# A fused two-layer decoder: weights of the first cross attention loaded a stage earlier, clearing and loads moved behind first rows, matrix products placed in waits

## The reference, cut to what matters

```python
x = x + L0_attn(_layernorm(x))            # 16 heads of 64, causal softmax, biases
x = x + L0_xattn(_layernorm(x), ctx)      # 16 heads of 16, softmax over 361 keys
x = x + L0_ffn(_layernorm(x))             # mixture: 2 of 8 experts of 704, and a shared one of 352
x = x + L1_attn(_layernorm(x))            # 16 heads of 16, linear: no softmax
x = x + L1_xattn(_layernorm(x), ctx)      # 16 heads of 64, softmax over 361 keys
x = x + L1_ffn(_layernorm(x))             # mixture: 8 of 64 experts of 128, and a shared one of 256
```

## Time and profile before

| | us |
|---|---|
| median of three runs | 3454.67 |
| the three runs | 3448.93, 3454.67, 3457.12 |
| the profiled execution, as timed | 3452.34 |
| its span in the trace | 3450.6 |
| busy: PE, PEld, DVE, ACT, POOL | 3254.7, 2422.0, 1887.5, 1646.8, 783.8 |

### The profile page before, as it was taken

One profiled execution on the slowest core, in us unless ns is written; L12 is line 12 of the kernel. 1 busy time (PEld: TensorE's weight loads), 2 busy tenths in 40 slices (PEclk: granted clock), 3 DMA queues, 4 the chain that ended last, 5 costly groups with the idle time before them and its releaser, 6 DMA issues. The chain is left out here.

```text
span 3450.6 us, 76147 instructions
## 1 busy us (share of the span) xinstructions
PE 3254.7 (94%) x24554; PEld 2422.0 (70%) x24555; DVE 1887.5 (55%) x5145; ACT 1646.8 (48%) x4614; POOL 783.8 (23%) x854
## 2 busy tenths in 40 slices
PE   8999999899999989899998989999999999998992
PEld 6777776566666656677776766777777777766871
DVE  4655555577777756122222664666666666663433
ACT  4555555566666611122222326666666666652220
POOL 1000000000000000333332110132332332336774
PEclk9999999899999989999999999999999999999996
DMA  8500000400000051211112100010000000025784
GB/s 274 151 0 0 0 0 0 157 9 11 11 11 11 5 161 43 77 30 31 30 29 46 52 0 5 16 43 21 18 14 11 15 13 12 13 81 141 203 221 137
DMA packets 136407, 181.28 MB, mean 53 GB/s; under 512 B 36156, under 2 KB 108601, under 8 KB 135308
## 3 DMA queue, kind: packets, MB, share of 16 engines
q1 hardware_dynamic: 84112, 133.96, 12.6%
q0 software_dynamic: 45760, 26.67, 4.8%
q10 hardware_dynamic: 6460, 19.66, 1.5%
HBM read 116.11 MB, written 103.61 MB: 64 GB/s over the span
## 5 line engine op out<-in xcount | busy, mean ns | idle before, releaser
L1269 DVE TENSOR_REDUCE e_nmx<-PS 128x1 f32<-128x361 f32 x416 | 221.3, 532 | 343.4 <-PE PS L1117 337.5
L1622 ACT ACTIVATE b_p<-PS,b_nmx 100x361 f32<-100x361 f32 x512 | 267.1, 568 | 148.4 <-DVE b_nmx L1704 148.4
L1117 PE MATMUL PS<-e_cT,e_qT 128*128 128x361 f32 x832 | 333.4, 483 | 0.0
L893 POOL DMA_INDIRECT slot_rows<-r_row,r_rows_now x256 | 256.7, 1003 | 336.7 <-DVE e_p L1276 290.2
L1221 ACT ACTIVATE e_pT<-PS 121x384 f32<-121x384 f32 (+1 forms) x416 | 199.0, 479 | 220.9 <-PE PS L1124 220.8
L2637 PE MATMUL PS<-c_wgu,c_tile_xT 128*128 x912 | 291.2, 463 | 1.4 <-ACT c_tile_xT L2692 1.4
L1704 DVE TENSOR_REDUCE b_nmx<-PS 100x1 f32<-100x361 f32 x512 | 243.5, 525 | 44.6 <-PE PS L1468 44.6
L1124 PEld LDWEIGHTS PS<-ident,e_p 128*121 128x121 f32 x1248 | 198.0, 184 | 96.2 <-ACT e_pT L1221 0.4
L1226 ACT ACTIVATE e_p<-PS,e_nmx 128x361 f32<-128x361 f32 x416 | 232.4, 559 | 36.3 <-DVE e_nmx L1269 36.2
L1475 PEld LDWEIGHTS PS<-ident,b_p 100*121 100x121 f32 x1536 | 188.5, 185 | 61.2 <-ACT b_pT L1606 31.0
L1475 PE MATMUL PS<-ident,b_p 100*121 100x100 f32 x1536 | 223.5, 280 | 6.5 <-ACT b_pT L1606 4.4
(11 more groups left out here) (338 smaller groups left out, 6462.9 us busy)
## 6 DMA issues: line engine op xcount, KB each, us to landing
f_w<-in_f_W SPq DMA_DIRECT2D x64, 384.0 KB, 3.7
slot_rows<-a_empty SPq DMA_DIRECT2D x1, 21504.0 KB, 65.3
f_xg<-slot_rows SPq DMA_DIRECT2D x64, 336.0 KB, 3.9
c_wgu<-in_c_GU ACTq DMA_DIRECT2D x8, 1408.0 KB, 16.6
sum<-X SPq DMA_DIRECT2D x2, 3200.0 KB, 57.0
f_sums<-sum SPq DMA_DIRECT2D x16, 400.0 KB
b_cT<-in_ctx_T SPq DMA_DIRECT2D x32, 181.5 KB, 2.3
e_cT<-in_ctx_T SPq DMA_DIRECT2D x32, 181.5 KB, 2.3
```

The costliest lines, as they stand in the source:

```text
L893: pool.indirect_dma_start(out=self.rows, in_=self.row[:, u, :], in_offset=None, out_offset=bass.IndirectOffsetOnAxis(ap=self.rows_now[:, u ...
L1117: sr.fill_done(pe.matmul(sr.at(f"s{m}", ROWS, CTX), qT[:, at:at + ROWS], cT[:, u, 0:CTX], start=True, stop=True), f"s{m}")
L1269: dve.tensor_reduce(nmx[:, m:m + 1], sr.at(f"s{m}", ROWS, CTX), AX.X, ALU.max, negate=True).then_inc(max_ready, 1)
L1622: sr.move_done(act.activation(p[:, g % 2, a, 0:CTX], sr.at(f"s{g}{a}", S, CTX), ACT.Exp, bias=nmx[:, g, a:a + 1]), f"s{g}{a}")
```

## The change

The change has five parts.

First, the weights, the first two contexts and their semaphores of `tiled_cross_attention` move into a class `TiledWeights`, placed on the right side of the on-chip memory. SP issues their six loads at the end of its program in `self_attention`, behind the wait for `slots_cleared`.

Second, in `tiled_cross_attention` POOL does the first root and waits for the two normalised batches before it clears v and p; the waits for `prepared` on PE and DVE move behind the first scores; ACT's eight loads of `c_wgu` are spread over the start of the stage (`load_ahead`). In `packed_cross_attention` POOL makes the routing's constants behind the first normalised pair.

Third, in `dispatch_and_shared` DVE takes the statistics of batches 4 to 6, then normalises pairs 0 and 1, and only then does the statistics of 7 to 15 and the variances of 4 to 15.

Fourth, the loads of experts 4 to 7 of `c_wd` move from step 35 to the start of `tiled_experts`, where SP issues them once the first gather has landed, ahead of `behind.load`.

Fifth, `keep_busy` puts products of the identity with itself, whose result nobody reads, on PE at the start of six stages: 6 in a_, 8 and 4 in b_, 9 in `dispatch_and_shared`, 18 in `tiled_experts`, 11 in d_ and 8 in e_.

The six removed lines at 1396 to 1401 are those of `load` and are cut here.

```diff
...
+def keep_busy(pe, k, bank, n):
+    for _ in range(n):
+        pe.matmul(k.PS[:, bank, 0:128], k.ident[:], k.ident[:], start=True, stop=True)
 def layer_norm_rstd(pool, ln, t):
     pool.wait_ge(ln.var_ready, t + 1)
-def self_attention(k, w):
+def self_attention(k, w, behind):
...
                 sp.wait_ge(k.slots_cleared, 16)
+                behind.load(sp)
...
                             project("k", 1, i)
+                keep_busy(pe, k, 7, 6)
                 turn(-1, False, True)
...
                 layer_norm_rstd(pool, ln, 0)
+                pool.wait_ge(ln.xn_ready, 2)
                 r.make_constants(pool)
                 layer_norm_rstd(pool, ln, 1)
                 pool.wait_ge(loaded, LOADED)
...
                             mr.pass_over_in(pe, i, *[name for name, at in routed.items() if at == n])
+                keep_busy(pe, k, 5, 8)
                 pe.wait_ge(loaded, LOADED)
                 pe.wait_ge(prepared, PREPARED)
-def tiled_cross_attention(k, w, name, ahead_to, ahead_from, ahead_loaded):
-    nc, X = k.nc, k.X
+class TiledWeights:
+    LOADED = 4 * 16
+    def __init__(self, k, ctx, w, name):
+        def sb(n, shape):
+            return ctx.enter_context(k.nc.sbuf_tensor(f"{name}_{n}", shape, F32, side="right"))
+        self.k, self.w, self.name = k, w, name
+        self.wq, self.wk = sb("wq", [128, KC, D]), sb("wk", [128, D])
+        self.wv, self.wo = sb("wv", [128, D]), sb("wo", [128, KC, D])
+        self.cT = sb("cT", [128, 2, 363])
+        self.loaded = k.sem(f"{name}_loaded")
+        self.ctx_loaded = [k.sem(f"{name}_ctx_loaded{u}") for u in range(2)]
+    def load(self, sp):
+        w, loaded = self.w, self.loaded
+        sp.dma_start(self.wq[:], w["Wq"].rearrange("(c p) n -> p c n", p=128)).then_inc(loaded, 16)
+        sp.dma_start(self.wk[:], w["Wk"]).then_inc(loaded, 16)
+        for u in range(2):
+            sp.dma_start(self.cT[:, u], self.k.ctx_T[u]).then_inc(self.ctx_loaded[u], 16)
+        sp.dma_start(self.wv[:], w["Wv"]).then_inc(loaded, 16)
+        sp.dma_start(self.wo[:], w["Wo"].rearrange("(t p) n -> p t n", p=128)).then_inc(loaded, 16)
+def tiled_cross_attention(k, tiled, ahead_to, ahead_from, ahead_loaded):
+    nc, X, name = k.nc, k.X, tiled.name
...
-        wq, wk = sb("wq", [128, KC, T * 128]), sb("wk", [128, T * 128])
-        wv, wo = sb("wv", [128, D]), sb("wo", [128, KC, D])
+        wq, wk, wv, wo, cT = tiled.wq, tiled.wk, tiled.wv, tiled.wo, tiled.cT
-        cT = sb("cT", [128, 2, KEYS * CH])
...
-        loaded, prepared, parity_made = sem("loaded"), sem("prepared"), sem("parity_made")
-        ctx_loaded = [sem(f"ctx_loaded{u}") for u in range(2)]
+        loaded, ctx_loaded = tiled.loaded, tiled.ctx_loaded
+        prepared, parity_made = sem("prepared"), sem("parity_made")
...
                 mr.wait_full(sp, "v02", -1)
                 sp.dma_start(cT[:, 0], k.ctx_T[2]).then_inc(ctx_loaded[0], 16)
                 with sp.Fori(0, TURNS - 2) as i:
-            LOADED = 64
+            LOADED = tiled.LOADED
             PREPARED = 2
             @block.gpsimd
             def _(pool):
+                layer_norm_rstd(pool, ln, 0)
+                pool.wait_ge(ln.xn_ready, 2)
                 pool.memset(v[:], 0.0).then_inc(v_cleared, 1)
                 pool.wait_ge(v_cleared, 1)
                 pool.memset(v[:, :, :, :, A:A + 1], 1.0).then_inc(prepared, 1)
                 pool.memset(p[:, :, :, CTX:KEYS * CH], 0.0).then_inc(prepared, 1)
-                with pool.Fori(0, TURNS + 1) as t:
+                with pool.Fori(1, TURNS + 1) as t:
                     layer_norm_rstd(pool, ln, t)
             @block.tensor
...
+                keep_busy(pe, k, 6, 8)
                 pe.wait_ge(loaded, LOADED)
-                pe.wait_ge(prepared, PREPARED)
                 mr.pass_over(pe, "v10", "v12")
                 turn_x(-1)
+                keep_busy(pe, k, 6, 4)
                 keys(0, 0, -1)
                 mr.pass_over(pe, "r0", "t0")
                 queries(-1)
...
                 values(0, 0, -1)
                 scores(1, 0)
                 values(0, 2, -1)
+                pe.wait_ge(prepared, PREPARED)
                 for a in range(TILES_R):
                     turn_probs(0, a, 0)
                 keys(1, 0, -1)
             @block.scalar
             def _(act):
-                act.wait_ge(loaded, 64)
-                for e in range(8):
+                def load_ahead(e):
                     act.dma_start(ahead_to[:, e].rearrange("p a c n -> p (a c n)"), ahead_from[e]).then_inc(ahead_loaded, 16)
...
                 move_queries(0, -1)
                 move_queries(1, -1)
                 move_keys(0, 1, -1)
+                load_ahead(0)
+                load_ahead(1)
                 act.wait_ge(prepared, PREPARED)
                 for g in range(2):
                     for a in range(TILES_R):
                         exponent(g, a, 0)
+                    load_ahead(2 + g)
                 move_probs(0, 0, 0)
                 move_probs(0, 2, 0)
+                load_ahead(4)
                 move_keys(1, 0, -1)
                 for a in range(TILES_R):
                     exponent(2, a, 0)
+                load_ahead(5)
                 move_probs(1, 0, 0)
                 move_probs(1, 2, 0)
+                load_ahead(6)
                 move_keys(1, 1, -1)
                 for a in range(TILES_R):
                     exponent(3, a, 0)
+                load_ahead(7)
                 move_probs(2, 0, 0)
                 move_probs(2, 2, 0)
                 with act.Fori(0, TURNS - 1) as i:
...
                 statistics(0)
                 apply(0)
-                dve.wait_ge(prepared, PREPARED)
                 for a in range(TILES_R):
                     maximum(0, a, 0)
+                dve.wait_ge(prepared, PREPARED)
                 move_values(0, 0, -1)
                 for a in range(TILES_R):
                     maximum(1, a, 0)
...
                         mr.pass_over(pe, "y1")
+                keep_busy(pe, k, 4, 11)
                 pe.wait_ge(loaded, LOADED)
                 turn(-1, False, True)
...
                         store_unit(j - 1)
-                    if n == TABLED_AT:
-                        sp.wait_ge(summed, B // GB)
-                        for e in range(len(LOAD_AT), E):
-                            sp.dma_start(d.wd[:, e].rearrange("p t n -> p (t n)"), routed["D"][e]).then_inc(d.wd_loaded[1], 16)
                 store_unit(UNITS - 1)
...
                         pe.sem_inc(xb.filled[xb.bank["table"]], 1)
+                keep_busy(pe, k, 7, 9)
                 pe.wait_ge(loaded, 16)
                 for n in range(STEPS):
...
                 statistics(*GROUPS[0])
                 variances(0)
-                statistics(*GROUPS[1])
-                variances(1)
+                statistics(4, 7)
                 apply(0)
                 apply(1)
+                statistics(7, 16)
+                variances(1)
                 choosing, listing = [choose(ch) for ch in range(2)], tile_list()
...
             @block.sync
             def _(sp):
+                sp.wait_ge(gathered[0], 16)
+                for e in range(4, d.E):
+                    sp.dma_start(d.wd[:, e].rearrange("p t n -> p (t n)"), routed["D"][e]).then_inc(d.wd_loaded[1], 16)
                 behind.load(sp)
...
                     yb.fill_done(last, "y")
+                keep_busy(pe, k, 7, 18)
                 turn_x(0, 0, 16)
                 pe.wait_ge(wgu_loaded, d.E * 16)
                 pe.wait_ge(cleared, 2)
...
-        self_attention(k, w["L0_attn"])
+        xattn_stage = ExitStack()
+        tiled = TiledWeights(k, xattn_stage, w["L0_xattn"], "b")
+        self_attention(k, w["L0_attn"], tiled)
         with nc.sbuf_tensor("c_wgu", [128, 8, 2, KC, 704], F32) as wgu:
             wgu_loaded = sem("c_wgu_loaded")
-            tiled_cross_attention(k, w["L0_xattn"], "b", wgu, w["L0_experts"]["GU"], wgu_loaded)
+            with xattn_stage:
+                tiled_cross_attention(k, tiled, wgu, w["L0_experts"]["GU"], wgu_loaded)
```

More of the change, by code:

```diff
@@ L1394, in load @@
                       .then_inc(ctx_loaded[u], 16)
-                sp.dma_start(wq[:], w["Wq"].rearrange("(c p) n -> p c n", p=128)).then_inc(loaded, 16)
-                sp.dma_start(wk[:], w["Wk"]).then_inc(loaded, 16)
-                for u in range(2):
-                    sp.dma_start(cT[:, u], k.ctx_T[u]).then_inc(ctx_loaded[u], 16)
-                sp.dma_start(wv[:], w["Wv"]).then_inc(loaded, 16)
-                sp.dma_start(wo[:], w["Wo"].rearrange("(t p) n -> p t n", p=128)).then_inc(loaded, 16)
                 mr.wait_full(sp, "v02", -1)
```

## The result

The changed kernel took 3439.9 us (median of eight runs, 3437.9 to 3450.6) against 3454.5 of the kernel before, measured beside it (eight runs). The ratio is 0.9966, 95% interval [0.9957, 0.9975]: 11.7 us faster, between 8.6 and 14.9; the 14.6 us between the two medians stand near the upper end of that. Forecast were 3440 us and 14.4 us. The sum came out within the interval; its terms did not, and one of them had the wrong sign.

The account below looks back on a forecast made before the run. PE, busy 94% of the span, bounds the kernel; gains come from its idle time and low-clock products at stage starts. 5.0 + 2.2 + 5.0 + 0.5 + 1.7 = 14.4 us gives 3440 us, range 3430 to 3449.

Parts of the forecast that it names:

- tiled_experts: Start of that stage: first gather lands sooner, `c_wd` by 1400.0, second tile's products 5.0 us earlier than 1405.12.
- F: Rival: two starts' gains are given back within the stage, as DVE or ACT sets the pace; 7.2 us remains, 3447.5; chance 0.05.
- tiled_cross_attention: Start of that stage: keys come sooner; 6.6 us gained if the clock holds, 3.4 if not, middle 5.0 taken.
- ACT's eight issues: First two turns of `tiled_cross_attention`: the `load_ahead` issues cost ACT 4.0 us, charged at 2.1, bounds 1 and 4.
- dispatch_and_shared: Start of that stage: pair 2's store goes sooner, so pair 4 and the shared expert's products come 2.2 us earlier.
- The price of `c_wd`: Start of `tiled_experts`: the four loads, issued behind the first gather, take 9.3 us from issue to landing.
- Rival D: `tiled_experts`: `c_wd` meets gathers, row adds and `d_` loads, takes twice 9.3 us; loses 4.2 us, 3449.5 us; chance 0.06.
- Rival G: `tiled_experts`: first gather shares with others anyway, lands at the median 4.6 us; start gives 3.3 us, total 3442.0; chance 0.08.
- linear_attention: Start of that stage: 11 products end before X comes; 1.9 us if they hold the clock, 0.5 taken.
- packed_cross_attention: Start of that stage: 0.45 us from the normalising step and 1.3 from the projections' clock, 1.7 in all.
- self_attention: First products of that stage: 1.4 us if the clock held, else nothing; the low value, 0, taken.
- B: Rival at the stage starts: the products of the identity never hold the clock; 10.45 us gained, 3444.2 us; chance 0.20.

Follow-up runs that it names:

- d_after_wd: The changed kernel with SP holding the next stage's loads until `c_wd` has landed; 0.9961 of the kernel before.
- before: The kernel before the change, its first profiled execution; median of eight runs 3454.5 us.
- before_again: The kernel before, unchanged, profiled once more; 3445.9 us, a single run.
- hold_alone: The kernel before with one line: SP issues the next stage's loads in `tiled_experts` only once the first gather has landed; ratio 1.0000.
- wd_back_hold: The changed kernel with the four `c_wd` loads back at step 35, the next stage's loads still behind the first gather; 3431.0 us, 0.9940 of the kernel before.
- products_alone: The kernel before with the products of the identity at the same places and nothing else; 0.9998 of the kernel before.
- hold_and_more: wd_back_hold with 12 more products of the identity in `dispatch_and_shared`, between pair 0's logits and pair 2's transposes; 0.9939 of the kernel before.
- again: The changed kernel, unchanged, measured once more; 3441.5 us, 0.9968 of the kernel before.
- stats_back: The changed kernel with DVE's old order in `dispatch_and_shared`, all statistics and variances before pairs 0 and 1; 0.9958 of the kernel before.

## Why the prediction was right, and where it was wrong

**The bound and the method** held. The gains lie at the starts, the steady turns are unchanged. By starts and lengths the change gives 8.3 + 3.3 - 2.7 + 0 + 2.2 = 11.1 us, against a forecast of 5.0 + 2.2 + 5.0 + 0.5 + 1.7 = 14.4 and measured ratios worth 11.7, 11.0 and 10.1 us. The `tiled_experts` term is the stage's mean in six executions, 492.5 us, against 489.8 in two of the kernel before. That the whole came so near is luck: +3.3 and +1.1 in two terms stand against -7.7 in a third. And that the first medians differ by 14.6 us, 0.2 from the forecast, is luck on top of it. The chance of faster, put at 0.87, is 0.885 by its own parts, with half of F in it, and that of the same 0.085; this changes nothing else.

**`tiled_cross_attention`, forecast 5.0, measured 8.3** (611.4 in three executions with the old start, 603.1 in eight with the new; 8.9 at the scores of the same executions). The steps held: transposes 3.1 us into the block (forecast 3.2), keys 4.4 (4.6), clearing hidden, weights there. I took the middle between a kept and a fallen clock; it was kept every time. The second misjudged term is ACT's eight issues, charged with 2.1 us: the stage gains nearly what the scores gain, 0.6 less, and the executions scatter by more than that. So no cost of the spread issues can be seen, while in one piece they put the first exponent 2.7 us later.

**`dispatch_and_shared`, forecast 2.2, measured 3.3.** Pair 0 came 3.8 us sooner (4.0). Pair 2 was normalised 11.6 us into the block, as forecast. The next step was too long: I had pair 4 come 4.43 us behind pair 2's store, as in the earlier trace rows; it came 3.2 us behind (1214.82 to 1217.98). Before, SP issued three more transfers in the 2 us behind that store, and now one; that they made the difference is likely, but no run shows it.

**`tiled_experts`, forecast +5.0, measured -2.7: the step that failed.** The gather's part was right (PE 5.6 us into the block, forecast 5.35). The price of `c_wd` was not. I took its landing, 9.3 us, from a place where it ran beside the end of dispatch (the trace has 10.0 there), and moved it to one where gathers run: 12.8 us by `d_after_wd`, 11.5 to 13.1 in the others. I left out the 1.3 to 1.5 us from the landing to PE's first product, which the old order hid. And I had no term for the clock behind the wait for `c_wd`, where it fell in that wait: 1.6 to 2.7 us, all in the second tile. The text named the point from which the part loses, 14.4 us; landing and loop entry together are 12.9 to 14.4, just at it, and the clock took the rest. The start of the profiled execution of before was also an unlucky one: its second tile came at 19.7, in `before_again` at 16.8, so 5.0 us were counted from the late end of what the old kernel does. Rival D came nearest, with a late landing, but put it at 18.6 us. Of the neighbours that it blamed, the loads of `d_` are cleared by `d_after_wd`; the gathers remain, not shown. The other fault is one of cause: I named both `c_wd` and the next stage's loads as what held the first gather and credited the package. With the products in place the hold had the whole gain; by itself, in `hold_alone`, it gave the whole kernel nothing that could be measured.

**Rival G**, by the Trainium skill's page "DMA: Bandwidth & Descriptors", section "Queues, rings and completion order": the first gather was there 3.1 us after its issue (1376.55 to 1379.61), not at the median of 4.6, so its outcome did not come. With the loads held back there was nothing to take turns with: the DMA engines moved 42 GB/s in these 3.1 us, which is the gather's own 128 KB. The rule itself isn't contradicted: turns between queues would hold a gather behind 1.2 MB as well as a queue in common does, and no run tells the two apart.

**The small terms.** `linear_attention`: forecast 0.5, measured nothing (187.7 to 190.1 in all). The 11 products run at the low clock and the first projections at the full (1.62 us), but for `wd_back_hold`, where they took 3.01. Yet the stage is not shorter; the executions scatter by more than the term. `packed_cross_attention`: the normalising step went to 0.74 and the transposes came 3.07 us into the block, 0.44 sooner (0.45), and the clock gave about 1.8 (1.3). `self_attention`: nothing, as taken; the first products took 3.00 us with the six products in front of them. Of the identity product the price was wrong: 0.24 us at full clock and 0.46 to 0.48 at the low (nine in 4.18 us), where I had 0.2 and 0.3 to 0.4. In dispatch the nine ended 0.50 us before the first rows came; a tenth might have been in the way. They gave nothing either: without them the shared expert begins at 17.2 us too.

**B**, that the products never hold the clock, was wrong as a whole, but right for the start of `tiled_cross_attention` in `products_alone`: what they do depends on the wait around them.

## What to carry to other kernels

When a load is moved off one transfer's way, look at what runs where it goes: its landing time belongs to its neighbours, not to its size. When a change bundles a hold with a move, price them apart; here the one-line hold gave 4.4 us beside the other parts, and the move that came with it lost 8. And set a stage's old length by more than one execution. Fill a wait with spare products only once it is nearly as short as they are, and judge a part of a few us by offsets from its block's start, for stage lengths and whole times carry clock stretches of 3 us each that come and go.

## What the runs showed of the hardware

The granted clock can be low while PE is busy throughout (8.00 of 8 us at 0.57 on average, 1291 to 1299 us). It was so once or twice, beginning 50 to 95 us into `dispatch_and_shared`, in twelve of the fourteen profiled executions, at 2.8 to 3.5 us each time. Ahead of the stretch at 1291 us PE had not been busy throughout. It had waited 2.35 us for DVE's choice of the experts:

```profile
1289.47 0.46 PE L2310 MATMUL PS<-c_sel,earlier 100*100 100x128 f32 x2 [2.35 <-DVE c_chosen L2449]
```

All fourteen executions have this wait, and two of them, `before` and `hold_and_more`, kept the clock behind it. The earlier one of the two stretches in `again` and `stats_back`, 51 and 54 us into the block, comes before it. So this wait stands in front of twelve of the fourteen stretches but doesn't settle them; what does stays open, and no run was made that shortens the wait.

Of the four loads of `c_wd`, the last piece was out for 2 to 3 us after the DMA engines had gone nearly quiet. And the same changed kernel took 3441.5 and 3473.9 us on two chips, 0.9% apart, nearly all of it in `packed_cross_attention` (1024.0 and 1044.4 us) and the last stage (357.7 and 372.3), while the kernel before moved with it, so only ratios compare across chips.
